# Second layer of a transformer sandwich: residual and norm between its blocks moved from token-major to feature-major tiles

## The reference

```python
x = x + _layernorm(attn(_layernorm(x)))     # layer 1: q, f, v, a scan over tokens, RMS norm, Wo
x = x + _layernorm(ffn(_layernorm(x)))      # layer 2

def ffn(x):                                 # layer 2, six blocks of 256 -> 1024 -> 256
    for i in range(6):
        x = gelu(x @ W1[i].T + B1[i]) @ W2[i].T + B2[i] + x
        if i < 5:
            mu = mean(x, -1); var = mean((x - mu)**2, -1)
            x = (x - mu) * rsqrt(var + 1e-5) * LN_G[i] + LN_B[i]
    return x
```

## Time and profile before

| | us |
|---|---|
| median of three runs | 699.8 (697.39, 699.8, 699.84) |
| profiled execution | 697.43 |
| its span, first to last instruction | 695.6 |
| PE busy in the span | 657.7 |
| PEld, DVE, POOL, ACT busy | 592.7, 412.6, 365.8, 351.8 |

### The profile page before, as it was taken

The page is one execution under the profiler, slowest core; times in us unless marked ns, Lnnn a source line. Parts: engine busy times, 40 slices in busy tenths (PEclk is TensorE's granted clock), DMA queues, the critical chain, the costliest instruction groups (busy, mean ns, idle before and its releaser), DMA issues.

```text
span 695.6 us, 11045 instructions
## 1 busy us (share of the span) xinstructions
PE 657.7 (95%) x4144; PEld 592.7 (85%) x4144; DVE 412.6 (59%) x847; ACT 351.8 (51%) x563; POOL 365.8 (53%) x443
## 2 busy tenths in 40 slices
PE   1979899998999999999999999999999999999994
PEld 1768688978999999999999999999999999999994
DVE  5899997795954454455435543564365445545554
ACT  3556475655555445445454454454464444444441
POOL 4567775369865755356365445562486255323111
PEclk9999999999999999999999999999999999999997
DMA  7120000000020022000050000210010000000001
GB/s 269 61 84 32 0 1 1 1 1 30 1 101 15 2 65 80 1 1 1 0 137 9 1 1 1 84 62 1 0 61 1 1 1 1 1 1 32 32 15 46
DMA packets 10421, 21.51 MB, mean 31 GB/s; under 512 B 1408, under 2 KB 6400, under 8 KB 10368
## 3 DMA queue, kind: packets, MB, share of 16 engines
q1 hardware_dynamic: 9792, 20.28, 9.0%
q10 hardware_dynamic: 576, 0.52, 0.2%
HBM read 18.70 MB, written 2.10 MB: 30 GB/s over the span
## 4 chain that ended last, share of the span: by engine, by line
PE 79%; DVE 11%; issue 4%; POOL 3%; ACT 1%; DMA 1%; SPq 0%; DVEq 0%; POOLq 0%; ACTq 0%
PE BK L357 38%; PE BK L531 37%; DVE R L325 3%; PE BK L336 3%; DVE SB L428 2%; PE BK L446 2%; DVE ST L311 1%; POOL R L486 1%; DVE OL L437 1%; DMA R<-in_wq 1%; POOL SB L455 1%; DVE R L473 1%; POOL QB L431 1%; DVE KB L425 1%; DVE HL L521 1%
## 5 line engine op out<-in xcount | busy, mean ns | idle before, releaser
L515 ACT ACTIVATE HH<-BK,B 128x512 fp32r<-128x512 f32 x192 | 132.2, 689 | 233.4 <-PE BK L357 232.1
L521 DVE TENSOR_TENSOR HL<-BK,HH 128x512 fp32r<-128x512 f32 x192 | 131.1, 684 | 179.4 <-ACT BK L518 179.4
L531 PE MATMUL BK<-WH,HH 128*128 128x256 f32 x768 | 217.3, 283 | 0.0
L531 PE MATMUL BK<-WL,HH 128*128 128x256 f32 x768 | 217.2, 283 | 0.0
L531 PE MATMUL BK<-WH,HL 128*128 128x256 f32 x768 | 216.8, 282 | 0.0
L357 PE MATMUL BK<-XH,WL 128*128 128x512 f32 x432 | 175.1, 405 | 4.0 <-DVE XL L344 3.3
L357 PE MATMUL BK<-XL,WH 128*128 128x512 f32 x432 | 171.2, 396 | 0.0
L357 PE MATMUL BK<-XH,WH 128*128 128x512 f32 x432 | 169.6, 392 | 0.0
L531 PEld LDWEIGHTS BK<-WH,HL 128*128 128x128 f32 x768 | 146.6, 191 | 8.1 <-issue 0.3
L531 PEld LDWEIGHTS BK<-WL,HH 128*128 128x128 f32 x768 | 146.6, 191 | 7.1
L531 PEld LDWEIGHTS BK<-WH,HH 128*128 128x128 f32 x768 | 146.6, 191 | 0.0
(11 more groups left out here) (61 smaller groups left out, 648.6 us busy)
## 6 DMA issues: line engine op xcount, KB each, us to landing
STG<-in_w SPq DMA_DIRECT2D x24, 512.0 KB, 3.6
out<-R SPq DMA_DIRECT2D x16, 128.0 KB, 1.9
X<-in_x SPq DMA_DIRECT2D x3, 512.0 KB, 8.2
GB<-in_b SPq DMA_DIRECT2D x6, 128.0 KB, 6.2
GB<-in_lng SPq DMA_DIRECT2D x5, 128.0 KB, 3.7
GB<-in_lnb SPq DMA_DIRECT2D x5, 128.0 KB, 4.7
R<-in_wv SPq DMA_DIRECT2D x1, 512.0 KB, 6.5
STG<-in_wo SPq DMA_DIRECT2D x1, 512.0 KB, 6.9
```

The lines of the kernel that those rows point to most:

```text
L515: lambda e, ev=ev, hs=hs, bias=bias: e.activation(HH[:, hs, :], bank_of[ev][:, :], ACT.Gelu, bias=bias),
L521: lambda e, ev=ev, hs=hs: e.tensor_tensor(HL[:, hs, :], bank_of[ev][:, :], HH[:, hs, :].bitcast(f32), ALU.subtract), ("hlo", n, j))
L531: r = e.matmul(dst, s, w, start=(j == 0 and c % 2 == 0 and i == 0), stop=(j == 7 and i == 2), skip_group_check=True)
```

## The change

In layer 2 the residual and the norm stay feature-major, in `R[:, t, :, k * 128:(k + 1) * 128]` (`feat(t, k)`).

`mm2` swaps its operands: a 128x128 piece of W2 is stationary and HH or HL moves with 512 columns, so a group takes six matmuls and the accumulator holds features x tokens. `y` adds B2 as a number per partition and the residual in one instruction for each half.

The mean over features now runs across partitions. GpSimd adds the two halves (`sum1`), VectorE transposes each 32x32 block of the sum (`tr1`) and adds up runs of 32 (`red1`, 128x16), PE multiplies that by a constant 128x128 matrix SEL that adds the four partition groups, divides by 256 and spreads the result (`mu`, a product of fp32 with 16 columns), and VectorE reads it from the bank with another block transpose that copies each value over 32 places (`mub`, into MB). VectorE subtracts it from both halves (`ctr`), ScalarE squares them (`sqr`), and `sum2`, `tr2`, `red2`, `va` follow in the same way for the variance; `vae` adds epsilon, GpSimd takes the power (`rsd`, 128x16), `rsb` spreads it, `nn` multiplies by it and by LN_G, ScalarE adds LN_B and writes XH, VectorE writes XL. LN_B is also folded into B2 of the next block, once, so that R needs no LN_B. The eight transposes of the step on PE are gone.

The ring gives `mu` and `va` a bank each time, as it gave one to each `turn`. `mm1` no longer takes BK4 and BK5 (`kept`). On the way into layer 2 the `turn` of the tile stays, and ScalarE makes one more copy of each half, from the bank to R (`xn`), ahead of XL. The steps of the last block turn back to token-major with eight transposes each, into the accumulator pair or, in the last step, into four free banks, with statistics, power and scaling read from there, chunk by chunk. The last step no longer splits its last `mm2` into two halves by token; its `y` is cut in four pieces of 256 columns. LN_G, LN_B and B2 come in by three small DMAs, in place of 16 of 128 KB.

```diff
+    def kept(who):
+        return shut | set(range(RING, RING + EARLY)) if who[0] == "mm1" else shut
...
+                if name == "l3":
+                    op("scalar", key + gap * k + 1.3, [ev, ("after", ("xhi", name, t, k))],
+                       lambda e, k=k, ev=ev: e.activation(feat(t, k), by_chunk(bank_of[ev][:, :]), ACT.Copy),
+                       ("xn", t, k))
...
+            op("gpsimd", E + 1.5, [("y", n, 0), ("y", n, 1), *before("tr1")],
+               lambda e: e.tensor_tensor(by_chunk(SA[:, :]), feat(t, 0), feat(t, 1), ALU.add), ("sum1", n))
+            op("vector", E + 3.2, [("sum1", n), *before("red1")], lambda e: e.transpose(TB[:, :], SA[:, :]), ("tr1", n))
+            op("vector", E + 3.9, [("tr1", n)],
+               lambda e: e.tensor_reduce(P1[:, p, :], TB[:, :].rearrange("p (b f) -> p b f", f=32),
+                                         mybir.AxisListType.X, ALU.add), ("red1", n))
+            product(E + 4.8, [("red1", n), ("ldsel",)],
+                    lambda e, bank: e.matmul(bank[:, 0:16], SEL[:, :], P1[:, p, :], start=True, stop=True),
+                    ("mu", n), ("mub", n))
+            op("vector", E + 5.2, [("mu", n), *before("nn1")],
+               lambda e: e.transpose(MB[:, :].rearrange("p (b f) -> p b f", f=32),
+                                     bank_of["mu", n][:, 0:16].unsqueeze(2).to_broadcast([128, 16, 32])), ("mub", n))
+            for k in range(2):
+                op("vector", E + 6 + 0.7 * k, [("mub", n)],
+                   lambda e, k=k: e.tensor_tensor(feat(t, k), feat(t, k), by_chunk(MB[:, :]), ALU.subtract), ("ctr", n, k))
+                op("scalar", E + 7 + 0.7 * k, [("ctr", n, k), *before("red2")],
+                   lambda e, k=k: e.activation(by_chunk(SQ[:, k, :]), feat(t, k), ACT.Square), ("sqr", n, k))
...
+            op("gpsimd", E + 12.5, [("vae", n), ("mhalf",)] + before("rsb"),
+               lambda e: e.tensor_tensor(RN[:, :], VN[:, :], MH[:, :], ALU.pow), ("rsd", n))
...
-                        for i, (s, w) in enumerate(((ol, wh), (oh, wl), (oh, wh))):
-                            r = e.matmul(dst, s, w, start=(j == 0 and c % 2 == 0 and i == 0),
-                                         stop=(j == 7 and i == 2), skip_group_check=True)
+                    for k in range(2):
+                        a = 2048 + 256 * j + 128 * k
+                        wh, wl = WH[:, b % 2, a:a + 128], WL[:, b % 2, a:a + 128]
+                        for i, (w, h) in enumerate(((wl, HH), (wh, HH), (wh, HL))):
+                            r = e.matmul(ACC[acc][k][:, :], w, h[:, hs, :], start=(j == 0 and i == 0),
+                                         stop=(j == 7 and i == 2))
...
-                turn(E + 20, name, t, [("addb", n, 3)], ("mm1", n + 4, 7), 2.6)
+                layer_norm(E, n, b, t)
...
+                    for k in range(2):
+                        m = e.transpose(token(c)[:, 128 * k:128 * k + 128], feat(t, k)[:, c, :], ID[:, :])
```

More of the change, by code:

```diff
@@ L543, in sandwich @@
             E = f_key(8 * n + 7 + LAG) + 3.0
-            if n == 4 * NB - 1:
-                for h in range(2):
-                    def both(e, h=h):
-                        for f in steps2[8 - TAIL:]:
-                            r = f(e, chunks=(2 * h, 2 * h + 1))
-                        return r
-                    op("tensor", E - 2 + h, [*(x for j in range(8 - TAIL, 8) for x in (("hlo", n, j), ("ghi", n, j))),
-                                             ("after", ("mm2", n, 7 - TAIL))], both, ("end", h))
@@ L553, in sandwich @@
-            for h in range(2):
-                op("vector", E + 0.7 * h, [("end", h) if n == 4 * NB - 1 else ("mm2", n, 7), ("addb2", n)],
-                   lambda e, n=n, t=t, h=h, acc=acc: e.tensor_tensor(
-                       R[:, t, 2 * h:2 * h + 2, :].rearrange("p a n -> p (a n)"), ACC[acc][h][:, :],
-                       R[:, t, 2 * h:2 * h + 2, :].rearrange("p a n -> p (a n)"), ALU.add), ("y", n, h))
-            name = f"f{b}"
-            sp = 1.0 if n < 4 * NB - 4 else 0.3 if n < 4 * NB - 1 else 0.0
@@ new lines, in sandwich @@
+            last = n == 4 * NB - 1
+            parts = [[0, 1], [2, 3]] if last else [[0, 1, 2, 3]]
+            for i, part in enumerate(parts):
+                for k in range(2):
+                    lo, hi = part[0], part[-1] + 1
+                    op("vector", E + 0.7 * k + 0.9 * i, [("mm2", n, 7), ("ldb2",), ("bias",)],
+                       lambda e, t=t, k=k, acc=acc, b=b, lo=lo, hi=hi: e.scalar_tensor_tensor(
+                           feat(t, k)[:, lo:hi, :], by_chunk(ACC[acc][k][:, :])[:, lo:hi, :],
+                           BS[:, 2 * b + k:2 * b + k + 1], feat(t, k)[:, lo:hi, :], ALU.add, ALU.add),
+                       ("y", n, k, i) if last else ("y", n, k))
@@ new lines, in sandwich, with token, tr @@
+            if b < NB - 1:
+                layer_norm(E, n, b, t)
+                continue
+            def token(c, acc=acc, last=last):
+                return BK[c][:, 0:256] if last else ACC[acc][c // 2][:, (c % 2) * 256:(c % 2) * 256 + 256]
+            for c in range(4):
+                def tr(e, t=t, c=c, token=token):
+                    for k in range(2):
+                        m = e.transpose(token(c)[:, 128 * k:128 * k + 128], feat(t, k)[:, c, :], ID[:, :])
+                    return m
+                S = 1.3 if not last else 0.9
+                K = E + 2 + S * c
+                op("tensor", K, [("y", n, k, c // 2) if last else ("y", n, k) for k in range(2)], tr, ("ft", n, c))
+                seen = ("ft", n, c if last else c | 1)
+                op("vector", K + 0.5, [seen], lambda e, t=t, c=c, token=token: e.bn_stats(ST[:, t, c, :], token(c)),
+                   ("z_st", n, c))
+                op("vector", K + 0.9, [("z_st", n, c)],
+                   lambda e, t=t, c=c: e.bn_aggr(MV[:, t, c, :], ST[:, t, c, :]), ("z_mv", n, c))
+                op("gpsimd", K + 1.2, [("z_mv", n, c)],
+                   lambda e, t=t, c=c: e.tensor_scalar(VE[:, t, c:c + 1], MV[:, t, c, 1:2], EPS_LN, 1.0, ALU.add, ALU.mult),
+                   ("z_ve", n, c))
+                op("gpsimd", K + 1.3, [("z_ve", n, c), ("mhalf",)],
+                   lambda e, t=t, c=c: e.tensor_tensor(RS[:, t, c:c + 1], VE[:, t, c:c + 1], MH[:, 0:1], ALU.pow),
+                   ("z_rs", n, c))
+                op("vector", K + 2.0, [("z_rs", n, c), *(("ft", n, d) for d in range(4))],
+                   lambda e, t=t, c=c, token=token: e.tensor_scalar(R[:, t, c, :], token(c), MV[:, t, c, 0:1],
+                                                                    RS[:, t, c:c + 1], ALU.subtract, ALU.mult),
+                   ("z_nm", n, c))
+                eng = "gpsimd" if c % 2 else "vector"
+                op(eng, K + 2.5, [("z_nm", n, c)],
+                   lambda e, t=t, c=c: e.tensor_tensor(R[:, t, c, :], R[:, t, c, :], X[:, t, c, :], ALU.add),
+                   (f"fin{c % 2}", t, c))
+                load(K + 3, out[t][:, c, :], R[:, t, c, :], ("stored", t, c), [(f"fin{c % 2}", t, c)])
```

136 lines of the change are left out of this document (81 added, 55 removed), and 1 row of the table LASTS.

## The result

The changed kernel takes 680.2 us in the median of four runs (678.8 to 681.2), the kernel before 698.6 in the same comparison (696.8 to 699.8). The ratio is 0.974, with a 95% interval of 0.971 to 0.977: 18.4 us are gone, where the prediction had 6.9. The profiled execution took 681.2 us; its span is 679.4 us, against 695.6.

A forecast was written before the change was run, and what follows sets the result against it. PE's queue, operation by operation, was taken to bound layer 2. Terms -7.7 - 17.6 + 11.6 + 3.0 + 2.8 + 1.0 = -6.9 us gave 690.5 or 692.9, depending on the base; forecast 691.5, range 685 to 698.5.

The forecast's parts named there:

- `mm2` swapped: Layer 2's mm2: six 512-column matmuls cost 1.39 us in place of 1.43, over 192 groups -7.7 us.
- transposes of the turns: PE in layer 2: 40 groups of four transposes behind the norms vanish, 0.44 us each, -17.6 us.
- small products: PE in the new norm: 40 products mu and va cost 0.29 us each, +11.6 us.
- last block's transposes: PE in the last block's first three steps: turning back with eight transposes each costs +3.0 us.
- waits of PE: PE at mu and va: both chains ready 1.5 us early, so no waiting charged, 0 us.
- the end: After the last matmul: four pieces of y, statistics and chunkwise powers lengthen the tail by +2.8 us.
- way into layer 2: Stretch where layer 1 still runs: more copies and DVE work, two banks lost, fewer GpSimd adds, +1 us.
- The rival at 708: Norm in layer 2: scan-priced block transposes and ctr slowed by GpSimd make PE wait, +17 us, about 708; chance 0.14.
- the mixed stretch gains: Stretch with both layers: relieved GpSimd removes up to 3 us of waits, end costs 2.3, total -11, about 687.5; chance 0.12.
- The rival of weight loads: PE in layer 2: weight loads set the pace, so removing 1,152 saves many tens of us; chance 0.01.

The follow-up runs named there:

- swap alone: Kernel before with only mm2 changed to six 512-column matmuls, W2 stationary, values not the reference's: 682.5 us against 698.7, ratio 0.976.
- mu_later: Changed kernel with mu issued six matmuls later in each block's last step: 677.4 us against 698.6, ratio 0.969; again 678.1 us, ratio 0.972.

## Why the prediction was wrong

The direction was right, and so was the chain of causes. One step failed, and it carries 7.2 of the 9.3 us that lie between the forecast sum (-6.9) and the difference of the two spans (-16.2). The other terms are off by up to 4 us each and cancel to 2.1. The terms of the sum beside what the runs showed:

| term | predicted, us | measured, us | from |
|---|---|---|---|
| `mm2` swapped, 192 groups | -7.7 | -19.2 at 0.10 a group | 2.82 to 2.72 us |
| swap alone, whole kernel | -7.7 | -16.2 in the medians, -14.9 in the spans | swap alone |
| transposes of the turns, 40 groups | -17.6 | -19.0 | 0.475 us a group |
| small products, 40 | +11.6 | +10.6 | 0.265 us each |
| last block's transposes | +3.0 | +3.0 | steps of 22.69 and 22.77 us less 21.76, and 1.0 in the last |
| waits of PE | 0 | +3.9 | four block ends, 0.97 us each |
| the end | +2.8 | +2.0 | last matmul to end of span, 9.3 to 11.3 us |
| way into layer 2, to step 3 | +1.0 | -1.9 | 202.29 (swap alone) to 200.37 us |
| norm and end together | +0.8 | -1.3 in the spans, -2.3 in the medians | changed kernel against swap alone |

The rows from the transposes to the way into layer 2 add up to -1.4, close to the 1.3 us by which the two spans differ, but two small faults cancel in that. The end there is set against the kernel before; against the swap alone, whose own end takes 9.5 us, it is +1.8. And of the 40 groups three and of the 40 products four stand ahead of step 3, where the row on the way into layer 2 counts them too, 0.4 us in all. By stretches the difference to the swap alone is -1.9 us up to step 3, -2.2 from there to step 23, and +2.8 from there to the end. The whole is -14.9 - 1.3 = -16.2 us.

**The step that failed** is the first term: "Six matmuls of 512 columns have just the shape of `mm1`, so I charge them 1.39 us in place of 1.43." The 0.232 us behind it are not the price of a 512-column matmul but that of one behind 256-column ones, which in layer 2 of the kernel before every `mm1` is. In an unbroken row it is 0.227, for the new `mm2` and for the old `mm1`. Twelve matmuls at 0.227 are 2.72 us, so the group saves 0.10 and not 0.04. Half of the missing 0.06 is the new `mm2` at 1.36 in place of the 1.39 charged; the other half is `mm1`, whose change the prediction left at nothing without a reason. The bounds of 0.03 and 0.05 were set by the rounding of the rows, as if the price itself were certain. Over the twenty steps from step 3 to step 23 the swap alone brings 467.5 - 452.8 = 14.7 us, 0.092 for each of their 160 groups; the 0.008 missing are the transposes, which have become dearer by 0.035 a group of four and stand twice in most steps. The remaining 32 groups lie in stretches where PE has idle time or at the end, and give 0.2 us together.

The evidence stood in the trace of the kernel before, in a place that I had not read, since it is not where layer 2 runs alone. At 92 to 97 us, where layer 1 still runs, PE has a long row of 512-column matmuls (PE's timeline of the kernel before, L357):

```profile
94.65 0.39 PE L357 MATMUL BK<-XH,WL 128*128 128x512 f32 x1
...
95.78 0.39 PE L357 MATMUL BK<-XH,WH 128*128 128x512 f32 x1
...
96.92 0.39 PE L357 MATMUL BK<-XL,WH 128*128 128x512 f32 x1
```

From 94.65 to 96.92 are ten intervals, 2.27 us, or 0.227 each. The right question to the trace was not "how long does this shape take?" but "how long does it take in the surroundings that it will have?".

**The transposes and the small products** were priced well from the earlier trace rows. The first are 0.035 us dearer, for they now break up a quick row; the second cost 0.265 in place of 0.29, since two instructions take 0.14 and not 0.20 us, and the slow followers add 0.035 that the prediction did not have.

**The waits of PE** were put at nothing and cost 3.9 us, the largest miss after the first term. The rival at 708, in which block transposes cost like the scan, did not come true either. Groups of the changed kernel (busy us, mean ns of one | idle before):

```profile
L556 POOL TENSOR_TENSOR RN<-VN,MH 128x16 f32<-128x16 f32 x20 | 58.3, 2913 | 57.5 <-DVE VN L554 57.5
...
L541 DVE TENSOR_TENSOR R<-R,MB 128x512 f32<-128x512 f32 x40 | 32.1, 841 | 0.7
...
L529 DVE STREAM_TRANSPOSE TB<-SA 128x512 f32<-128x512 f32 x20 | 14.1, 703 | 3.5 <-POOL SA L528 3.5
...
L548 DVE TENSOR_REDUCE P<-SQ 128x16 f32<-128x512 f32 x20 | 13.7, 684 | 0.6
...
L662 POOL TENSOR_TENSOR RS<-VE,MH 128x1 f32<-128x1 f32 x16 | 9.1, 578 | 0.9
```

The block transpose takes 0.70 us and the reduction 0.68, against 0.68 forecast and 1.315 at the other bound. The rule of the Trainium skill that I had set beside it (Vector Engine (DVE) Microarchitecture Reference, "The reshape front-end and per-opcode configuration") is borne out by this trace, 0.703 us for 512 elements of a lane. The subtraction `ctr` is at 0.84 in the mean, above the 0.70 assumed: it takes 0.69 alone and up to 1.78 beside a weight piece. The power on 16 columns takes 2.91 us. The prediction had no price for it, and it does not hurt: it stands behind `va`, where PE waits for nothing. The slack was thinner than forecast, though. In a usual step `red1` is ready 7.81 us after the start of the last `mm2` matmul, where 7.0 were forecast, and PE comes for it at 8.39; `red2` is ready 7.85 us after `mu`, where 6.9 were forecast, and PE comes at 8.43. So some 0.6 us were to spare in place of 1.5, in part because DVE holds an `hlo` that waits for its gelu ahead of `tr1`. At the four block ends the slow XL add 1.4 us to the first chain, and PE waits. The prediction had both sources in view, "At block boundaries `sum1` stands behind pieces of the weight split" for the way into layer 2, and the slowing of DVE beside GpSimd for a rival. The first did not happen (`sum1` waited for `y` and not for a piece), and the second was given no price at the later blocks.

**The end** came out at +2.0 us, and the last add, now one of GpSimd's, ends 8.5 us after the last matmul's end, where 8.4 to 9.7 were forecast. The stretch of the end in the changed kernel (L632 `y`, L659 and L662 epsilon and power, L670 the last adds):

```profile
668.09 0.39 PE L614 MATMUL BK<-HL,WH 128*128 128x512 f32 x1
...
668.52 1.66 DVE L632 SCALAR_TENSOR_TENSOR R<-BK,BS,R 128x256 f32<-128x256 f32 x4 [3.48 <-PE BK L614]
...
671.02 0.19 POOL L659 TENSOR_SCALAR VE<-MV 128x1 f32<-128x1 f32 x1 [7.08 <-DVE MV L657]
...
672.47 1.33 POOL L662 TENSOR_TENSOR RS<-VE,MH 128x1 f32<-128x1 f32 x2
...
676.29 0.72 POOL L670 TENSOR_TENSOR R<-R,X 128x256 f32<-128x256 f32 x1 [0.66 <-DVE R L665]
```

The power on one column takes 0.578 us (in the rows above, between 0.35, from which I got 2.3, and 1.0). The chain runs as forecast through the four pieces of `y` (1.66 us) and GpSimd's powers, of which the last is held up behind an addition (673.95 to 674.67 us in the trace).

**The way into layer 2** was to cost 1 us. Against the swap alone it gained 1.9 up to step 3. This is what the rival "the mixed stretch gains" has for this stretch. The measure is weak, though: the first `mm2` starts at 103.7 to 108.1 us across all the traces of kernels with the new norm, 104.0 and 105.5 in two executions of `mu_later`, while PE's order up to there is the same. It goes with the granted clock, which lies between 0.66 and 1.00 in stretches of 10 us from 30 to 80 us: where its mean over the first 100 us is 0.97 the first `mm2` starts at 103.7 to 105.5 us, and where it is 0.91 to 0.95, at 105.5 to 108.1. From the first `mm2` to step 3 the changed kernel takes 93.6 us, the same in both of its traces and in those of `mu_later`, and the swap alone 97.2. With the old `mm2` the norm shortens this stretch too, from 97.5 to 94.5 us. The gain of the stretch itself is thus nearer to 3.6 us. Which of the waits there it comes from, no run takes apart.

**The rival of weight loads**, in which they set the pace and many tens of us go, stays excluded: 1,152 loads are gone and PEld falls from 85% to 78%, and the starts are 0.227 us apart where a load takes 0.19. In the smaller sense it is open, as said: whether it is the width or the extra loads of the narrower matmuls that makes those behind them slow.

## What to carry to other kernels

Read the price of a matmul from start to start in the surroundings in which it will stand, and look for such surroundings in the whole trace, other stages included; where the same instruction shows two prices, find out what stood ahead of it before either goes into a sum. A change of one instruction's shape can also change what its neighbours cost: here 0.03 of the 0.10 us of a group were saved on matmuls that the change does not touch. When an in-order engine gets a new wait, check its slack at the irregular places too (here the ends of blocks, where another engine does extra work), since the usual step shows none of it, and half a group of later issue took away most of it.

## What the hardware showed

- A 512-column matmul starts every 0.227 us in an unbroken row of such, and every 0.232 for five intervals after 256-column ones or after the one that follows a transpose; after a small product nine intervals have a mean of 0.231. The Trainium skill (TensorE: Matmul & The Clock Gate, "Back-to-back issue gap") gives about 0.216 us for 512 columns as the isolated gap and about 0.131 for a steady stream with loads; the traces here don't agree with the second, since no 512-column matmul was followed closer than 0.22 us. Why the interval is longer after a narrow one is not shown, nor whether it is its width or its extra weight load that does it. After four small instructions in a row in place of two the followers were quick at once, and this, too, is open.
- Two instructions of a small fp32 product take 0.14 us and four 0.36: the first starts 0.03 us before the next, the others take 0.11 each.
- The fp32 block transpose of 128x512 costs 0.70 us, hardly more than a subtraction, also where its input is a 16-column read from PSUM spread over 512 elements (0.704 us for `mub`).
- An instruction of DVE on 128x512 that reads two operands in SBUF took 0.74 us with GpSimd idle (XL, 30 of them) and 1.27 or 1.78 beside a weight piece (ten). One that reads a bank and SBUF (`hlo`) took 0.68 beside the same pieces, and a block transpose 0.71.
- GpSimd's power takes 2.91 us for 16 columns, 1.03 for four and 0.58 for one.
